# A message table of the source product alone, with the edge type's term added to the gathered rows from one-hot products

## What is computed

```python
def _L3_gnn_ref(x, edge_index, edge_type, edge_emb_W, msg_W, msg_b, upd_W, upd_b, ln_g, ln_b):
    src = edge_index[0]
    dst = edge_index[1]
    et = edge_emb_W[edge_type]
    m_in = jnp.concatenate([x[src], et], axis=-1)
    m = jax.nn.relu(m_in @ msg_W.T + msg_b)
    agg = jax.ops.segment_sum(m, dst, num_segments=x.shape[0])
    deg = jax.ops.segment_sum(jnp.ones_like(dst, dtype=x.dtype), dst, num_segments=x.shape[0])
    agg = agg / jnp.clip(deg, 1.0)[:, None]
    out = agg @ upd_W.T + upd_b
    h = x + out
    ...
```

## Time and profile before

| what | us |
|---|---|
| median of 3 runs | 6097.74 |
| lowest, highest | 6093.89, 6148.96 |
| the profiled execution | 6144.82 |
| its span in the trace | 6143.1 |
| busy: PE, DVE, ACT, POOL | 3264.6, 3419.6, 1743.9, 3514.1 |

### The profile page before, as it was taken

One profiled execution on the slowest core, in us unless ns is written; L12 is line 12 of the kernel. 1 busy time (PEld: TensorE's weight loads), 2 busy tenths in 40 slices (PEclk: granted clock), 3 DMA queues, 4 the chain that ended last, 5 costly groups with the idle time before them and its releaser, 6 DMA issues.

```text
span 6143.1 us, 57856 instructions
## 1 busy us (share of the span) xinstructions
PE 3264.6 (53%) x17251; PEld 1781.1 (29%) x17252; DVE 3419.6 (56%) x4001; ACT 1743.9 (28%) x2410; POOL 3514.1 (57%) x2519
## 2 busy tenths in 40 slices
PE   1322222222214658776335887699999944444444
PEld 0222122112211222222333222244454423333333
DVE  5576766766756988997898899711101051111111
ACT  0000000000003448887444888700101151000001
POOL 0277777777777888888888860000000006777775
PEclk6555555555557777888655779899999975555555
DMA  9422222222227963333896333377677642222222
GB/s 411 136 1 1 1 1 1 1 1 1 1 1 273 350 209 89 99 83 85 293 318 201 90 96 86 92 268 277 225 257 246 234 146 75 52 52 52 52 52 50
DMA packets 448447, 760.76 MB, mean 124 GB/s; under 512 B 273523, under 2 KB 354666, under 8 KB 408678
## 3 DMA queue, kind: packets, MB, share of 16 engines
q1 hardware_dynamic: 278372, 702.23, 33.8%
q0 software_dynamic: 163840, 54.71, 9.6%
q10 hardware_dynamic: 6146, 2.68, 0.2%
HBM read 552.67 MB, written 187.47 MB: 120 GB/s over the span
## 4 chain that ended last, share of the span: by engine, by line
PE 24%; issue 20%; POOL 19%; DVE 14%; DMA 12%; ACT 3%; SPq 1%; POOLq 1%; DVEq 0%; ACTq 0%
PE PS L651 20%; POOL edge_weight_and_count L594 14%; POOL tiles L625 6%; DVE tiles L1522 5%; DVE feature_major L1468 4%; DMA tiles<-edge_weight_and_count 4%; DVE tiles L1515 3%; DMA edge_weight_and_count<-weight_and_count,target 3%; DMA tiles<-message_table,gather_index 2%; DMA copies_then_records<-edge_count 2%; PE PS L844 1%; PE PS L773 1%; PE PS L963 1%; DMA message_table<-tiles 1%; ACT copies_then_records L1093 1%
## 5 line engine op out<-in xcount | busy, mean ns | idle before, releaser
L625 POOL DMA_INDIRECT tiles<-message_table,gather_index x808 | 775.0, 959 | 1676.9 <-DMA message_table<-tiles 1430.9
L594 POOL DMA_INDIRECT edge_weight_and_count<-weight_and_count,target x784 | 1241.3, 1583 | 622.6 <-issue 255.8
L614 POOL DMA_INDIRECT sorted_edges<-record_slot,place_slot x784 | 1390.2, 1773 | 276.8 <-issue 230.5
L651 PE MATMUL PS<-tiles 128*64 128x392 f32 (+1 forms) x3200 | 754.8, 601 | 246.1 <-DVE tiles L1522 243.2
L695 PE MATMUL PS<-consts,key_slot 128*128 128x128 f32 x798 | 195.6, 422 | 1200.7 <-DVE target L1352 1197.2
L651 PE MATMUL PS<-tiles,node_major 128*128 128x448 f32 (+1 forms) x2100 | 812.6, 547 | 10.8 <-ACT node_major L1024 10.7
L963 PE MATMUL PS<-tiles 128*128 128x128 f32 x1616 | 491.6, 460 | 538.4 <-DMA tiles<-message_table,gather_index 538.4
L1522 DVE SCALAR_TENSOR_TENSOR tiles<-tiles,copies_then_records 128x1568 f32<-128x1568 f32 (+1 forms) x400 | 703.0, 1785 | 113.3 <-ACT tiles L1127 97.7
L1468 DVE SCALAR_TENSOR_TENSOR feature_major<-tiles,s,feature_major 128x1600 f32<-128x1600 f32 (+3 forms) x384 | 679.6, 1844 | 37.9 <-ACT tiles L1080 37.7
L1682 DVE TENSOR_TENSOR tiles<-lane_row,edges 128x1024 f32<-128x1024 f32 x101 | 123.6, 1226 | 877.2 <-PE PS L963 871.6
L963 PEld LDWEIGHTS PS<-tiles 128*128 128x128 f32 x1616 | 374.7, 322 | 655.8 <-issue 655.8
(11 more groups left out here) (253 smaller groups left out, 3016.9 us busy)
## 6 DMA issues: line engine op xcount, KB each, us to landing
tiles<-edge_weight_turned SPq DMA_DIRECT2D x72, 1568.0 KB, 6.9
tiles<-edge_count SPq DMA_DIRECT2D x72, 1568.0 KB, 7.9
tiles<-edge_weight_and_count SPq DMA_DIRECT2D x48, 1600.0 KB, 8.7
edge_weight_and_count<-feature_major SPq DMA_DIRECT2D x48, 1568.0 KB, 39.3
copies_then_records<-edge_count SPq DMA_DIRECT2D x192, 392.0 KB, 3.2
tiles<-edge_weight_and_count SPq DMA_DIRECT2D x48, 1536.0 KB, 8.9
edge_weight_turned<-copies_then_records SPq DMA_DIRECT2D x48, 768.0 KB, 4.8
edge_count<-copies_then_records SPq DMA_DIRECT2D x24, 800.0 KB, 4.6
```

The source lines that it names most:

```text
L594: nc.gpsimd.indirect_dma_start(out=edge_d, out_offset=bass.IndirectOffsetOnAxis(ap=idx[:, s, a:a + 1], axis=0), in_=pay[:, s, a, :], in_of ...
L614: nc.gpsimd.indirect_dma_start(out=rec_d, out_offset=bass.IndirectOffsetOnAxis(ap=place_slot[:, s, a:a + 1], axis=0), in_=rec_slot[:, s, a ...
L625: nc.gpsimd.indirect_dma_start(out=msg[:, s, a, :], out_offset=None, in_=table_d, in_offset=bass.IndirectOffsetOnAxis(ap=gs[:, s, a:a + 1] ...
L651: return nc.tensor.matmul(out_ap, lhsT, rhs, start=start, stop=stop)
```

## The change

The table holds the source product alone: 3136 rows, written in seven pieces as PE and ACT finish them. The type goes with the edge: the record's key now holds 256 x type beside the destination lane; DVE takes the two apart between the second and the third aggregation of L2, PE transposes the types (7 transposes) and they go to DRAM as bf16 in sorted order. In the gather, SP loads for each turn the types of its 1024 edges into 96 partitions (`load_types`, one DRAM row read 96 times), DVE compares them with the partition's number (`type_hot`), and PE multiplies that one-hot by a stack of three bf16 parts of the type terms into one PSUM bank of four chunks (`add_types`). DVE adds the bank to the gathered rows of two slots, ACT takes the relu in place (`make_messages`), and PE sums as before. POOL's gathers are the same 808, from the smaller table.

```diff
@@ SP, in the three streams of the count matrix
             for j in range(3):
+                if j == 1:
+                    for s in range(2):
+                        sp.wait_ge(S(f"records_sorted{s}"), 8 * EC)
+                    sp.dma_start(wrec[:, :].bitcast(I32), rec_d.rearrange("(p c) k -> p (c k)", p=TP)).then_inc(S("records_loaded"), 16)
                 stream(count_m, k)
@@ SP, after the last stream
-            for s in range(2):
-                sp.wait_ge(S(f"records_sorted{s}"), 8 * EC)
-            sp.dma_start(wrec[:, :].bitcast(I32), rec_d.rearrange("(p c) k -> p (c k)", p=TP)).then_inc(S("records_loaded"), 16)
-            for j in range(TYPES):
-                sp.wait_ge(S("table_made"), j + 1)
-                sp.dma_start(table_d[j * NP:(j + 1) * NP, :].rearrange("(p t) n -> p t n", p=TW),
-                             tab[j % 3]).then_inc(S(f"table_out{j % 3}"), 16)
+            sp.wait_ge(S("type_steps"), 3)
...
+            def load_types(i):
+                sp.dma_start(type_rows[i % 3], types_d[i * HOT:(i + 1) * HOT, :].rearrange("c p -> (c p)").unsqueeze(0)
+                             .to_broadcast([TYPE_ROWS, HOT * TP])).then_inc(S(f"types_in{i % 3}"), 16)
+            for i in range(3):
+                load_types(i)
+            for b in range(CH):
+                sp.wait_ge(S("msg_x_copied"), b + 1)
+                sp.dma_start(table_d.rearrange("(p t) n -> p t n", p=TW)[:, 4 * b:4 * b + 4, :],
+                             msg_x[:, 4 * b:4 * b + 4, :]).then_inc(S("table_out"), 16)
+            for i in range(3, TURNS):
+                sp.wait_ge(S("type_steps"), MARKS + i - 2)
+                load_types(i)
@@ POOL
-            for s in range(3):
-                pool.wait_ge(S(f"table_out{s}"), 16 * ((TYPES + 2 - s) // 3))
+            pool.wait_ge(S("table_out"), 16 * CH)
@@ PE, layer norm 6 and the products
             layer_norm(6)
+            pe.wait_ge(S("type_steps"), 1)
+            for k in range(2):
...
+                    last = nc.tensor.transpose(SM[0:n, (b % 4) * TP:(b % 4 + 1) * TP], types[:, b * TP:b * TP + n], ident)
+                last.then_inc(S("type_terms"), 1)
             pe.wait_ge(S("h3_ready"), 1)
-            pe.wait_ge(S("types_copied"), 1)
             for t in range(TN):
                 last = mm(bigT[0:TW, t, :], H[:, t:NP:TN], asel)
-            last.then_inc(S("msg_x"), 1)
-            pe.wait_ge(S("nm_ready"), NM_MSG)
-            for k in range(TYPES):
-                last = mm(bigT[0:TW, k, :], ident[0:TYPES, k:k + 1].to_broadcast([TYPES, TW]), type_part[:, :])
-            last.then_inc(S("msg_t"), 1)
+                if t % 4 == 3:
+                    last.then_inc(S("msg_x"), 1)
...
+            def add_types(slot, half):
+
+                for q in range(4):
+                    last = mm(SM[:, q * TP:(q + 1) * TP], type_hot[slot % 3][:, half * 4 + q, :], type_stack[:, :])
+                last.then_inc(S("type_terms"), 1)
@@ PE, sum_block
-                for s in range(4):
-                    slot = block % 2 * 4 + s
-                    pe.wait_ge(S(f"gathered{slot}"), (k + block // 2) * (16 * GM) + 16 * GM)
-                    for a in range(GM):
...
+                for half in range(2):
+                    if not (isinstance(i, int) and i == TURNS - 1 and half):
+                        pe.wait_ge(S("types_added"), i * 2 + (half + 1))
+                        if half:
+                            pe.wait_ge(S("type_steps"), i * 1 + (MARKS + 2))
+                        add_types(block + half, 1 - half)
+                    pe.wait_ge(S("messages_made"), i * 2 + (half + 1))
+                    for s in (2 * half, 2 * half + 1):
+                        for a in range(GM):
...
@@ ACT
-            A_(TR, bigT[0:TW, 0:TYPES, :], ACT.Copy).then_inc(S("table_types_copied"), 1)
-            for k in range(TYPES):
-                act.wait_ge(S("table_sum"), k + 1)
-                A_(tab[k % 3], tab[k % 3], ACT.Relu).then_inc(S("table_made"), 1)
...
+            for b in range(CH):
+                act.wait_ge(S("msg_x"), b + 1)
+                A_(msg_x[:, 4 * b:4 * b + 4, :], bigT[0:TW, 4 * b:4 * b + 4, :], ACT.Copy).then_inc(S("msg_x_copied"), 1)
+
+            def make_messages(i, half):
+                act.wait_ge(S("types_added"), i * 4 + (half + 1))
+                pair_of = msg[:, 2 * half:2 * half + 2, :, :]
+                A_(pair_of, pair_of, ACT.Relu).then_inc(S("messages_made"), 1)
@@ DVE
+            def read_types():
+                for k, n in enumerate((4, (NCH + TP - 1) // TP - 4)):
+                    dve.wait_ge(S("type_terms"), k + 1)
+                    o(v.tensor_copy(types_turned[:, 4 * k:4 * k + n, :], SM.rearrange("p (b n) -> p b n", n=TP)[:, 0:n, :]))
+                    signal("type_steps")
+            layer_norm(6, H, read_types)
...
-            for k in range(TYPES):
-                if k >= 3:
-                    dve.wait_ge(S(f"table_out{k % 3}"), 16 * (k // 3))
-                v.tensor_tensor(tab[k % 3], msg_x, TR[:, k, :].unsqueeze(1).to_broadcast([TW, TN, D]),
-                                ALU.add).then_inc(S("table_sum"), 1)
...
                 v.tensor_tensor(hot[:, i % 3, :, :], lane_row[:, :].unsqueeze(1).to_broadcast([TP, HOT, TP]),
                                 lane[:, group(i, HOT)].unsqueeze(2).to_broadcast([TP, HOT, TP]), ALU.is_equal).then_inc(S("lanes_made"), 1)
+                dve.wait_ge(S(f"types_in{i % 3}"), 16 * (i // 3 + 1))
+                v.tensor_scalar(type_hot[i % 3].rearrange("p b n -> p (b n)"), type_rows[i % 3], type_id[:, :], None,
+                                ALU.is_equal).then_inc(S("type_steps"), 1)
+                for half in range(2):
+                    dve.wait_ge(S("type_terms"), 2 * i + half + 3)
+                    slot = i % 2 * 4 + 2 * half
+                    for s in (slot, slot + 1):
+                        dve.wait_ge(S(f"gathered{s}"), (i // 2 + 1) * 16 * GM)
+                    v.tensor_tensor(msg[:, slot:slot + 2, :, :].rearrange("p s b n -> p (s b n)"), SM,
+                                    msg[:, slot:slot + 2, :, :].rearrange("p s b n -> p (s b n)"), ALU.add).then_inc(S("types_added"), 1)
```

More of the change, by code:

```diff
@@ L26 @@
 TYPES = 16
+TYPE_ROWS = 96
+TYPE_BITS = 8
+TYPE_STEP = 256
+MARKS = 4
 TP = 128
@@ L304, in graph_layers @@
         lane = edges[:, :, :].rearrange("p k c -> p (k c)")[:, 0:NCH].bitcast(F32)
[L305 to L307 removed]
+        types = edges[:, :, :].rearrange("p k c -> p (k c)")[:, NCH:2 * NCH].bitcast(F32)
         msg_x = fm[0:TW, 5 * NP:5 * NP + TN * D].rearrange("p (t n) -> p t n", t=TN)
@@ L311, in graph_layers @@
         msg = tiles[0:TP, 2 * TN * D:2 * TN * D + GS * GM * D].rearrange("p (s b n) -> p s b n", s=GS, b=GM)
-        assert 2 * TN * D + GS * GM * D <= 3 * NP and GS == 8 and TURNS % 2 and 3 * HOT * TP <= TN * D
+        type_rows = [tiles[0:TYPE_ROWS, 3072 + s * 512:3584 + s * 512].bitcast(BF16) for s in range(3)]
+        type_hot = [tiles[0:TYPE_ROWS, 4608 + s * 512:5120 + s * 512].bitcast(BF16).rearrange("p (b n) -> p b n", b=HOT)
+                    for s in range(3)]
+        types_turned = tiles[0:TP, 6144:6592].bitcast(BF16).rearrange("p (b n) -> p b n", n=TP)
+        assert 2 * TN * D + GS * GM * D <= 3 * NP and GS == 8 and TURNS % 2 and 3 * HOT * TP == 3072 and 6785 <= 2 * TN * D
         LN = [(X, Sf, Df, Df), (X, P2, P3, P3), (X, P2, P3, P3), (P1, P2, P3, P3), (P1, P2, P3, P3),
@@ L1185, in copy_parameters @@
                 o.add(A_(weT[:, :], SM[0:32, 256:384], ACT.Copy))
-                o.add(A_(embT[:, :], SM[0:32, 384:384 + TYPES], ACT.Copy))
+                for k in range(3):
+                    o.add(A_(embT[:, 32 * k:32 * k + TYPES], SM[0:32, 384:384 + TYPES], ACT.Copy))
                 o.done()
@@ L1264, in _ @@
                 index_slot(TURNS // 2 * GS + s, s)
+                if s % 2:
+                    make_messages(TURNS // 2 - 1, s // 2)
+            for half in (2, 3):
+                make_messages(TURNS // 2 - 1, half)
+            for half in (0, 1):
+                make_messages(TURNS // 2, half)
             layer_norm(7)
```

83 lines of the change are left out of this document (53 added, 30 removed).

## The result

The change made the kernel a little faster: the median of its runs is 6077.7 us (20 runs, 6047.7 to 6112.8) against 6102.9 us for the kernel before (20 runs, 6068.0 to 6149.0), a ratio of 0.9955 with an interval of 0.9934 to 0.9976. The ratio stands for some 27 us (the medians differ by 25), inside the 1% (61 us) that the prediction called no change, and beside a forecast of 34.

What follows compares the result with a forecast made beforehand. The prediction took the gather stage as bound by POOL alone, the table's stage by its 16 rounds. Terms: -91.6 + 0.5 + 54 + 2.7 = -34 us, so 6064 us; the forecast's own range 6048 to 6078.

Steps and rivals of the forecast that it cites:

- The table: Stage before the gathers: 16 rounds of sum, relu and write go, so the first gather starts 91.6 us earlier.
- The types in the layer norm: Last layer norm: seven transposes and two copies of types hidden with 0.3 us to spare, costed at 0.5 us.
- The gather: Gather stage: `hot` starts 0.70 us behind a gather, the next loses 0.55; 54 us over some 98 turns.
- the rule: Gather length: the larger of 0.955 us and (end of `hot` - start of the gather + 0.83).
- The first rival: Gather stage: POOL sits out `type_hot` as well, a turn loses 1.17 us, +27 us in all, 6124; chance 0.18.
- The second rival: Gather stage: `hot` and gathers keep in step as before, no long gathers, -88 us, 6010; chance 0.22.
- The third: Gather stage: late landings leave POOL without free slots, a turn costs 12 us, +104 us, 6200; chance 0.10.
- The tail: After the last landing: a sum, a relu, two more chunks and two wake-ups add 2.7 us.
- The base: Median of the runs before, 6097.7 us, to which the forecast difference was applied, giving 6064.

Runs made afterwards that it cites:

- the swapped order: Changed kernel with `type_hot` put ahead of `hot` on DVE, the work unchanged; 6367.1 and 6235.6 us on two other chips.
- The two moved versions: Changed kernel with the next turn's `hot` moved ahead of the first or the second sum of a turn; 6030.2 and 6026.7 us.
- the kernel before with the memset: Kernel before the change with a 128x512 memset put ahead of each `hot`, nothing else; 6320.2 and 6346.7 us on two other chips.

## Why the prediction was right

**The table.** Forecast -91.6, measured -92.9. ACT's last copy is 0.60 us long, as its row said. Between its end (4949.16) and the first gather lie 2.5 us, where I had put 3.7 for the landing of 224 KB between the two rows; that is the one difference, and it lies below the lower of the two.

**The types in the layer norm.** Costed at 0.5 with 0.3 us to spare; hidden, with more room. I had sized a transpose as a product of the same shape, 0.42 us; seven took 1.15 us, 0.16 each. The copies took what their nearest rows said (0.69, 0.56).

**The gather.** Forecast 54, measured 53.7, and step by step: `hot` starts 0.74 us behind a gather at the median (forecast 0.70), the gather after it loses 0.57 (forecast 0.55), in nearly every turn. The whole of it rested on one late `hot` in the trace of before and on the first gather; those two gave the rule and its 0.83. The two small misses go the same way: the second sum starts 0.14 behind a gather where I had 0.10. The sums cost the gathers nothing, as assumed: the 11 gathers of the changed kernel that began within one took 0.955 to 0.957 us, which the prediction had no row for. What I had not asked is how far ahead of a gather a `hot` must start to hold it; the last section has that.

**The first rival** (POOL sits out `type_hot` too) didn't come. Its mechanism is real, as the swapped order shows, but not at this boundary, and `type_hot` takes 476 ns, not the 0.7 us by which I priced it. With 0.48 us, POOL sitting it out would have cost a turn 0.97, just over the 0.9 from which it would have decided the sign.

The Trainium skill (VectorE: DVE Perf Modes, "The perf-mode tier table (the rule you actually need)") led to the estimate of 0.4 us by four elements a cycle; the row says 476 ns, so that estimate was nearer than the 0.7 of my nearest row.

**The second rival** (the two fall in step again) came in two turns, in which `hot` started 0.08 behind a gather. In the changed kernel nothing pulls it there: `hot` hangs on a sum that hangs on a landing, and the landing keeps its place. The two moved versions are this rival made by hand; they took 6030 and 6027 us where its price said 6010 from the median of three runs, and -83 and -87 us against before where it said -88.

**The third** (the ring runs dry) did not come where the change was timed; on the two chips with late landings it came as well to the kernel before with the memset, where POOL waited 98 and 88 us. The types' loads may show at the first sum of a turn, though no run singles them out: it starts 0.31 us behind a gather (0.22 to 0.56 between the tenths), the second 0.14 (0.07 to 0.19). That lateness costs nothing, since no `hot` follows it.

**The tail.** Forecast +2.7, measured +2.6, but the match is luck in part, for three differences add up to it. From the last landing to PE's last product it takes 3.6 us (6033.16 to 6036.72) where it took 1.2, which is +2.3 for what I had put at 2.7. The last landing itself comes 1.1 us sooner after the last gather's start (7.7 against 8.7). And the way from the last product to the end is 1.3 us longer: PE was granted 0.80 of full speed in the 17.3 us behind the last product, before 0.88 in 16.6. I had neither of the last two. (The last landings are 3.6 us apart in the earlier trace rows, not 3.4.)

**The base.** I subtracted the forecast from the median of three runs, 6097.7; twenty gave 6102.9. The predicted 6064 is 14 below the measured 6077.7, of which 5 are the base and the rest within the spread of executions.

## What to carry to other kernels

When one engine sets a stage by a chain of equal instructions, ask of each neighbour where in their beat it starts, not only how much it does: here 1.2 us of DVE work costs 0, 0.57 or 0.95 us a turn by its place alone. A single record that broke the beat in the trace of before gave the price of the whole stage. And an instruction with nothing left to wait for belongs right behind the start of what it would disturb: hang it on an event that already comes there, ahead of the instruction that would push it back.

## What the runs showed of the hardware

DVE and a gather on POOL get in each other's way at two places of the gather, and not with the same instructions at each.

- **Early**, at the gather's start. A gather that starts while a `hot`, with two inputs in SBUF, is running ends 0.83 us after it. As a gather takes 0.955 by itself, a `hot` that ends up to 0.13 us into it costs nothing. I take it that the read of the row numbers from SBUF is what waits; no row shows the read itself. Who comes first is not settled at 0.13 us: 144 `hot` in all traces started 0 to 0.13 us behind a gather's start, with no `type_hot` right ahead (L1682 in the earlier trace rows is one), and each of these gathers took 0.95 to 0.97. Where such a `hot` started within 0.02 us of the gather it was itself the longer one, 1.24 to 1.25 us. One that starts later, as at 5506.26 above, does nothing to the rest of the gather either. A `type_hot`, with one bf16 input and two-byte output, delays the gather in this way too: with `type_hot` behind the first sum, five gathers that began within one that had nothing behind it took 1.05 to 1.11 us, its end + 0.83.
- **Later**, from 0.48 to 0.72 us after the start, between the gather and `type_hot` alone; sums, memsets and `hot` started there kept their lengths. Beside a gather of the usual length, all 163 `type_hot` that started in that stretch ended 1.19 to 1.21 us after the gather's start, whatever their own start: 0.72 + 0.47, so that they waited for POOL and took up to 0.71 us instead of 0.47. Where one started a little earlier, at 0.39 to 0.48, it kept its 0.47 or 0.48 and the gather ended 0.12 us after it instead (0.98 to 1.07 us, 9 records). Both sides in the run with `type_hot` behind the first sum (L1753):

```profile
5612.95 0.96 POOL L650 DMA_INDIRECT tiles<-message_table,gather_index  x1 [0.30 <-ACT gather_index L1290]
5613.47 0.67 DVE L1753 TENSOR_SCALAR tiles<-tiles 96x1024 bf16<-96x1024 bf16 x1
...
5788.48 1.01 POOL L650 DMA_INDIRECT tiles<-message_table,gather_index  x1 [0.30 <-issue]
5788.90 0.47 DVE L1753 TENSOR_SCALAR tiles<-tiles 96x1024 bf16<-96x1024 bf16 x1
```

The first starts at 0.52 and ends at 1.19; the second starts at 0.42, ends at 0.89, and the gather at 1.01.

The Trainium skill (SBUF — State Buffer, "SBUF: two separate sides") puts such waits down to a pair of ports that DVE and GpSimd share, taken by whichever starts first "for the whole instruction", and says that GpSimd cannot write a DMA's descriptors without it; the later stretch would fit that last point, though no row shows what POOL does in it. The whole instruction doesn't agree on POOL's side: a gather is in the way at two short stretches of its 0.955 us only. `hot` from 0.18 on ran its 1.22 us beside the rest of it, and `type_hot` from 0.72 on its 0.47.
